# Dense stages of a four-layer graph network on one core: two operand buffers, statistics that run along, layer norms in three parts, and a Gelu on turned nodes

## The chip, the cores and the metric

The kernel runs on one core of a Trainium2 chip. Its time is the time on the device in microseconds (us), the median of several executions. The core has a matrix engine (TensorE, PE in the rows, with its weight loads as PEld), VectorE (DVE), ScalarE (ACT), GpSimd (POOL) and SyncE (SP, which here only starts transfers). Each engine works through its own queue in order and waits on counters (semaphores) of the others.

## The reference

Four graph layers follow each other on 6250 nodes of 128 numbers and 100,000 edges, each with a residual and a layer norm behind it. Cut to what matters here:

```python
x = _layernorm(x + L0(x, ...))   # edge means; three times relu(out @ W.T + b), then a batch norm over all nodes
x = _layernorm(x + L1(x, ...))   # relu((mean of neighbours + x) @ W.T + b)
x = _layernorm(x + L2(x, ...))   # messages [x[src], x[dst]] @ Wmsg[type]; mean; then the lines below
x = _layernorm(x + L3(x, ...))   # weighted sum of neighbours @ W, + b, relu, batch norm

# inside L2
h = jnp.concatenate([x, agg], axis=-1) @ Wupd + bupd
mu = jnp.mean(h, axis=-1, keepdims=True); var = jnp.var(h, axis=-1, keepdims=True)
hn = (h - mu) / jnp.sqrt(var + EPS) * gamma + beta
return x + jax.nn.gelu(hn, approximate=False)
```

A layer norm takes mean and variance over the 128 numbers of a node, a batch norm over the 6250 nodes of each column.

## The kernel before

**Data.** The nodes lie in `X` as 49 groups of 128 nodes: a node is a partition, its 128 numbers lie along it. A tile is one group, 128x128. Dense work goes in 7 steps (STEPS) of 7 tiles (STEP), 896 numbers wide. `A`, `B` and `sums` are three regions of one large buffer (`big` in the rows), `At` and `Bt` are views of the first two by group. `zr` and `zt` hold one step each; `zr2` and `zt2` are two more, inside `ring_raw`, which outside the dense stages is the ring of rows on their way from or to DRAM. PSUM (`ps`) has eight banks of 512.

**Stages.** The kernel sorts the edges into blocks of slots, then alternates: `gather` sends node rows to the blocks (PE with one-hot matrices, ACT, and POOL's scattering transfers), `reduce` sums blocks into nodes (SP's loads, DVE's one-hot matrices, PE, DVE's adds). Between a reduce and the next gather stands a dense stage. There are four:

- *First layer.* `edge_means` on DVE writes a step into `zr`. PE turns it (`turn`, seven transposes into banks 0 and 1, L1230), ACT copies the turned step to `zt` (`copy_t`, L826), PE multiplies halves of 448 columns into banks 2 and 3 (`mlp0`, L1237 and L1239), ACT applies bias and relu into `A` (`relu_cols`, L831), where nodes now lie turned, columns as partitions. `batch_norm` on DVE then takes 25 column statistics of 250 nodes (`column_stats`, L1666), joins them (L1676), ACT takes the square root (L836), four operations on one column each give scale and shift (L1680 to L1683), and one operation scales all of `A` (L1688). Two sublayers, mlp1 and mlp2 (L1253), do the same without the turning. In stage x1 ACT applies the last batch norm tile by tile into `zr` (L854), PE turns it back, DVE adds it to `X` (L1696) and takes each tile's norm statistics (L1607). `variances` (L1621 to L1627) and `scales` (L1635, L1636), with a square root on ACT between them (`ln_sqrt`, L869), give the factors, and DVE normalises 49 tiles (L1645).
- *f1 and g2.* f1 is the dense part of L1, g2 makes three messages per node for L2. f1: DVE's operands (L1726), turn, copy, product (`dense`, L1274), bias (L1733), relu and residual (L1735), statistics, and per step `variances` and `scales`. g2 follows two steps behind: ACT normalises a step into `zr2` (L900), turn, copy to `zt2` (L893), product (L1290) into banks 6 and 7 in turn, and DVE's add of the bias (L1750) into `msgs`, which SP writes to `msg_rows` step by step (L514). After the seventh of these transfers SP loads the first six lane rows into `zr` and `zt` (L522), from which DVE compares the one-hot matrices of the next gather (L1583).
- *f2 and Gelu.* f2: operands (L1791), turn, copy, product (L1274), add (L1798), statistics and per-step `variances` and `scales`; ACT normalises (L878), POOL multiplies by gamma and adds beta over 896 columns (L707, L709), ACT applies Gelu in a loop (L979), DVE adds it to the doubled node (L1821) and takes statistics.
- *f3 and x3*, the last layer: as mlp0 and x1, with the statistics already following the steps (L1848 for the operands, L1342 for the product); then the last norm, on DVE and ACT together, and the output.

The order within each engine is the order in which its part of the program is written.

## Time and profile before

| | us |
|---|---|
| median of 3 executions | 4178.9 |
| lowest and highest | 4169.08 and 4180.64 |
| the profiled execution | 4188.61 |
| its span, first to last instruction | 4186.9 |
| PE busy (matmuls) | 3063.3, 73% |
| DVE busy | 2712.8, 65% |
| POOL busy | 1880.8, 45% |
| ACT busy | 1166.1, 28% |

The busy shares are means over stages with different limits. Beside them the profile gives the busy time of each engine in a stretch of time (windows), the instructions in order of time (timeline) and groups of instructions by line. A row of the windows gives, behind the length, the busy time and the number of records of PE, PEld, DVE, ACT and POOL in this order, then the granted clock, the busy share of the DMA engines and GB/s. In a row of the timeline a time in brackets is idle time of the engine just before, with the instruction that ended it. Rows of the same line on the same engine that follow closely are merged, with their number as x7. A product in 32 bits appears as two records. The granted clock of PE is given in parts of 2.4 GHz: 1.00 is 2.4 GHz and 0.50 is 1.2 GHz.

### The profile page before, as it was taken

Reading aid. Unit: us, or ns where it says so; the run is one execution under the profiler, and the core shown is the slowest. Engines: PE = TensorE matmul, PEld = TensorE weight load, DVE = VectorE, ACT = ScalarE, POOL = GpSimd, SP = SyncE. Lnnn points to the kernel's source line nnn. Section 1 sums busy time; section 2 is a strip of 40 time slices with the busy share of each in tenths; the row PEclk is TensorE's granted clock in tenths of the full one; section 3 lists DMA queues with packets and bytes.
Section 4 is the critical chain, followed back from the end, with each engine's and each line's share of the span. In section 5 each row is a group of like instructions: output and inputs, shape, how many; then the busy total and the mean of one; then the engine's idle time right before and its main releaser. Section 6 shows DMA issues by size and latency. Waiting matters only on the chain.

```text
span 4186.9 us, 97803 instructions
## 1 busy us (share of the span) xinstructions
PE 3063.3 (73%) x24223; PEld 2679.1 (64%) x24224; DVE 2712.8 (65%) x7131; ACT 1166.1 (28%) x4154; POOL 1880.8 (45%) x1861
## 2 busy tenths in 40 slices
PE   7455444444388846998887799999989847998885
PEld 6233222222277616987877598899977837887883
DVE  6566766666577746665777644444467876666886
ACT  0111000000011125664112232222233047997004
POOL 3777777777600203775000166666633035773000
PEclk9999999999999977999999899999999978999997
DMA  6444444444477502444774354445466813445882
GB/s 192 145 140 145 147 144 142 147 146 140 126 240 243 162 0 88 174 180 154 235 226 153 129 150 145 147 148 153 119 186 203 257 32 128 173 178 178 252 253 76
DMA packets 423935, 667.68 MB, mean 159 GB/s; under 512 B 69406, under 2 KB 233641, under 8 KB 422873
## 3 DMA queue, kind: packets, MB, share of 16 engines
q1 hardware_dynamic: 330344, 431.37, 34.4%
q0 software_dynamic: 93552, 235.88, 15.7%
q8 instruction: 14, 0.23, 0.0%
q14 instruction: 25, 0.20, 0.0%
HBM read 418.34 MB, written 294.50 MB: 170 GB/s over the span
## 4 chain that ended last, share of the span: by engine, by line
PE 41%; POOL 20%; issue 14%; DVE 8%; DMA 7%; ACT 5%; DVEq 3%; SPq 2%; ACTq 1%; POOLq 0%
POOL slots L603 17%; PE ps L1147 15%; PE ps L1184 9%; PE ps L1188 9%; DVE hot_raw L1544 3%; ACT ring_raw L794 2%; DMA gbuf<-ring_raw,fetch_idx 2%; DMA ring_raw<-slots 2%; DMA ring_raw<-gbuf 2%; PE ps L1169 2%; PE ps L1030 2%; DVEq L409 1%; PE ps L1230 1%; POOL gbuf L649 1%; PE ps L1221 1%
## 5 line engine op out<-in xcount | busy, mean ns | idle before, releaser
L1147 PE MATMUL ps<-ring_raw,hot_raw 128*128 128x128 f32 (+2 forms) x8256 | 1012.6, 280 | 213.1 <-DVE hot_raw L1544 190.7
L1147 PEld LDWEIGHTS ps<-ring_raw,hot_raw 128*128 128x128 f32 x8256 | 966.2, 193 | 270.0 <-DVE hot_raw L1544 182.1
L649 POOL DMA_INDIRECT gbuf<-ring_raw,idx_blk x738 | 742.0, 1005 | 872.3 <-ACT fetch_idx L805 431.9
L603 POOL DMA_INDIRECT slots<-ring_raw,idx_edges x782 | 760.8, 973 | 240.9 <-issue 240.6
L1184 PE MATMUL ps<-big,hot_raw 128*128 x5328 | 613.9, 277 | 51.2 <-ACT ring_raw L797 28.7
L1184 PEld LDWEIGHTS ps<-big,hot_raw 128*128 128x128 f32 x5328 | 603.2, 193 | 62.4 <-issue 62.4
L1589 DVE TENSOR_SCALAR hot_raw<-ps,row_t 128x512 f32<-128x512 f32 x516 | 386.9, 750 | 262.3 <-PE ps L1169 260.8
L1555 DVE TENSOR_TENSOR big<-big,ps 128x128 f32 (+2 forms) x1032 | 292.4, 283 | 246.4 <-PE ps L1147 243.6
L1544 DVE SCALAR_TENSOR_TENSOR hot_raw<-ring_raw,back,lane_ids 128x512 f32<-128x512 f32 x516 | 386.1, 749 | 74.9 <-DMA ring_raw<-slots 40.8
L1062 PE MATMUL ps<-big 128*49 128x343 bf16 (+6 forms) x784 | 264.1, 490 | 206.3 <-DVE big L1444 205.2
L1544 DVE SCALAR_TENSOR_TENSOR hot_raw<-dst_key,back,lane_ids 128x512 f32<-128x512 f32 x516 | 388.8, 754 | 9.0 <-PE ps L1184 4.0
L1062 PEld LDWEIGHTS ps<-big 128*49 128x49 bf16 x784 | 113.9, 159 | 349.8 <-DVE big L1444 169.1
L1071 PE MATMUL ps<-big 49*128 49x98 f16 x784 | 159.7, 256 | 233.5 <-ACT big L729 233.5
L1188 PE MATMUL ps<-X,hot_raw 128*128 x2064 | 289.0, 283 | 24.7 <-DVE hot_raw L1589 16.8
L1188 PE MATMUL ps<-big,hot_raw 128*128 x2064 | 288.7, 283 | 23.7 <-ACT ring_raw L794 12.1
L794 ACT ACTIVATE ring_raw<-ps,pays_raw 128x128 f32<-128x128 f32 x1032 | 293.8, 375 | 0.0
L1583 DVE TENSOR_SCALAR hot_raw<-zr,row_t 128x512 f32<-128x512 bf16 x333 | 150.7, 507 | 214.9 <-PE ps L1184 208.3
L797 ACT COPY ring_raw<-ps 128x512 f32<-128x512 f32 x480 | 278.8, 583 | 0.0
L1188 PEld LDWEIGHTS ps<-X,hot_raw 128*128 128x128 f32 x2064 | 251.6, 192 | 31.7 <-issue 31.4
L1188 PEld LDWEIGHTS ps<-big,hot_raw 128*128 128x128 f32 x2064 | 251.3, 192 | 30.6 <-issue 30.4
L1071 PEld LDWEIGHTS ps<-big 49*128 49x128 f16 x784 | 103.4, 136 | 258.5 <-issue 258.5
L788 ACT COPY idx_blk<-to_blk 128x1 uint32 (+1 forms) x738 | 143.4, 194 | 436.6 <-PE ps L1184 266.1
(249 smaller groups left out, 3824.6 us busy)
## 6 DMA issues: line engine op xcount, KB each, us to landing
ring_raw<-gbuf SPq DMA_DIRECT2D x774, 268.0 KB, 3.3
ring_raw<-slots SPq DMA_DIRECT2D x258, 272.0 KB, 3.5
ring_raw<-in_edge_attr SPq DMA_DIRECT2D x111, 448.0 KB, 4.0
pays_raw<-key_rows SPq DMA_DIRECT2D x112, 224.0 KB
zr<-lane_rows SPq DMA_DIRECT2D x111, 128.0 KB, 3.6
zt<-lane_rows SPq DMA_DIRECT2D x111, 128.0 KB, 3.3
big<-src_rows SPq DMA_DIRECT2D x112, 112.0 KB
slots<-ring_raw,idx_edges POOLq DMA_INDIRECT x782
```

What stands on the lines that cost most here:

```text
L603: pool.indirect_dma_start(edges, bass.IndirectOffsetOnAxis(idx_edges[0:n, u, j:j + 1], 0), edge_rows[0:n, u, j, :], None).then_inc(scatter ...
L649: pool.indirect_dma_start(gbuf, bass.IndirectOffsetOnAxis(idx_blk[:, r:r + 1], 0), node_rows[:, r, :], None, bounds_check=NBLK - 1, oob_is ...
L794: ins = act.activation(rows[:, j, 0:D], parts[:, j, :], ACT.Copy, scale=pays_raw[:, bass.ds(at * (BLK * PAY) + (j * PAY + P_W), 1)])
L797: ins = act.copy(rows[:, :, 0:D], parts)
L1062: ins = pe.matmul(counts_of(s)[:, j * GROUPS:].rearrange("p (n g) -> p n g", g=GROUPS), hot2[:, s, 0, :, j], hot2[:, s, 1, :, j][:, None, ...
L1071: pe.matmul(to, hot, bases[:, s, 0, :], start=True, stop=False, skip_group_check=True)
L1147: ins = pe.matmul(bank(r % 3, width), hots[:, r, j * P:(j + 1) * P], rows[:, j, 0:width], start=j == 0, stop=j == BLK - 1)
L1184: ins = pe.matmul(to, hots3[:, r % 2, t, j * P:(j + 1) * P], msgs_flat[:, bass.ds(at[r] + t * D, D)], start=t == 0, stop=t == TYPES - 1)
L1188: ins = pe.matmul(to, hots[:, r, j * P:(j + 1) * P], nodes[:, bass.ds(at[r], D)], start=True, stop=True)
L1544: dve.scalar_tensor_tensor(out=hots[:, r, :].rearrange("p (k d) -> p k d", k=BLK), in0=key.broadcast_to([P, BLK, P]), scalar=back[:, k, ba ...
L1555: dve.tensor_tensor(to, to, bank(r % 3, width), ALU.add).then_inc(added, 1)
L1589: ins = dve.tensor_scalar(hots[:, r, :], bank(r % 3), row_t[:, 1:2], None, ALU.is_equal)
```

## The change

The gather and reduce stages stay as they are. In the dense stages:

1. mlp0 and f3 get two buffers for turned operands (`turned_to`: `zt` and `zt2`) and four product banks (2 to 5) instead of two; ACT's copy of the next step stands ahead of the relus of this one (`turned_layer`).
2. Column statistics of mlp0, mlp1 and mlp2 wait for the halves that they need (`columns_of`), and in mlp0 they stand between the operand sets (`layer_operands`), as in f3 before. The scaling of `A` is cut into 14 halves, each of which releases one product.
3. In x1 and x3 ACT applies the batch norm in one activation per step, into `zr` and `zt` in turn; PE turns into banks 0 to 1 and 2 to 3 in turn; DVE's statistics follow one step behind the adds. After x1 ACT normalises 3 of 7 tiles of each step, DVE 4.
4. The twelve turns of `lanes_t` and their copy stand between mlp1 and mlp2. POOL, not DVE, zeroes `sums` before the first graph layer.
5. The layer norms behind f1 and f2 take `variances`, square root and `scales` for steps 0 to 1, 2 to 4 and 5 to 6 (`CHUNKS`) and no longer per step. g2 follows three steps behind f1, not two.
6. SP loads the first six lane rows ahead of the last three transfers of messages.
7. POOL's multiply and add are gone. PE turns the normalised steps into PSUM (`z_turn`), ACT applies Gelu to them with gamma and beta as scale and bias columns (`cols[:, 13:15]`), PE turns them back (`g_turn`), and DVE adds them from PSUM. DVE normalises the last two steps.
8. Loops over the 7 steps are mostly written out.

Three places of the order. On DVE between the last operands of mlp0 and the statistics of mlp1, before:

```order
L1664 MEMSET big 128x6517 [waits mlp0_z]
L1666 BN_STATS bn_st<-big 128x6 [waits mlp0_r]
L1666 BN_STATS bn_st<-big 128x6 x24
L1676 BN_AGGR bn_mv<-bn_st 128x2 [waits vector_chain]
L1680 RECIPROCAL bn_c<-bn_c 128x1 [waits bnsd_in,bnsd_out]
L1681 TENSOR_TENSOR bn_c<-bn_c,cols 128x1 [waits vector_chain]
L1682 TENSOR_TENSOR bn_c<-bn_mv,bn_c 128x1 [waits vector_chain]
L1683 TENSOR_TENSOR bn_c<-cols,bn_c 128x1 [waits vector_chain]
L1688 TENSOR_SCALAR big<-big,bn_c 128x6272 [waits vector_chain]
L1666 BN_STATS bn_st<-big 128x6 [waits mlp1_r]
L1666 BN_STATS bn_st<-big 128x6 x24
```

and now:

```order
L1701 BN_STATS bn_st<-big 128x6 [waits mlp0_r] x4
L1697 TENSOR_SCALAR zr<-big,rcnt 128x128 [waits mlp0_t]
L1697 TENSOR_SCALAR zr<-big,rcnt 128x128 x6
L1701 BN_STATS bn_st<-big 128x6 [waits mlp0_r] x11
L1729 BN_AGGR bn_mv<-bn_st 128x2 [waits vector_chain]
L1733 RECIPROCAL bn_c<-bn_c 128x1 [waits bnsd_in,bnsd_out]
L1734 TENSOR_TENSOR bn_c<-bn_c,cols 128x1 [waits vector_chain]
L1735 TENSOR_TENSOR bn_c<-bn_mv,bn_c 128x1 [waits vector_chain]
L1736 TENSOR_TENSOR bn_c<-cols,bn_c 128x1 [waits vector_chain]
L1743 TENSOR_SCALAR big<-big,bn_c 128x448 [waits vector_chain]
L1743 TENSOR_SCALAR big<-big,bn_c 128x448 x13
L1701 BN_STATS bn_st<-big 128x6 [waits mlp1_r] x25
```

The memset is gone from DVE. The eleven last statistics of mlp0 wait one by one for its relus, and the 25 of mlp1 stand behind fourteen scaled pieces.

On ACT from the end of f2 (normalising `big`) through Gelu, before:

```order
L878 ACTIVATE big<-big,nmr,rstd 128x128 [waits f2_scaled]
L878 ACTIVATE big<-big,nmr,rstd 128x128 x6
L981 UNCONDITIONAL_BRANCH
L981 ISA
L979 ISA [waits norm_ready]
L979 ACT_TABLE_LOAD
L979 ACTIVATE big<-big 128x896
L981 REGISTER_ALU
L981 COMPARE_AND_BRANCH
L869 ACT_TABLE_LOAD
L869 ACTIVATE sd<-mv,eps_col 128x49 [waits mv_done]
```

and now:

```order
L882 ACTIVATE sd<-mv,eps_col 128x21 [waits mv_done]
L833 COPY zt<-ps 128x896 [waits f2_t,f2_m]
L894 ACTIVATE big<-big,nmr,rstd 128x128 [waits f2_scaled]
L894 ACTIVATE big<-big,nmr,rstd 128x128 x20
L882 ACTIVATE sd<-mv,eps_col 128x14 [waits mv_done]
L1013 ACT_TABLE_LOAD
L1013 ACTIVATE zr<-ps,cols 128x896 [waits z_turned]
L1013 ACTIVATE zt<-ps,cols 128x896 [waits z_turned]
L1013 ACTIVATE zr<-ps,cols 128x896 [waits g_turned,z_turned]
L1013 ACTIVATE zt<-ps,cols 128x896 [waits g_turned,z_turned]
```

The table load stands ahead of the first Gelu and no longer in a loop; the last square root stands behind 21 activations.

On SP, messages (`msg_rows`) and lane rows, before:

```order
L498 COMPARE_AND_BRANCH
L514 DMA msg_rows<-big 128x7x384 [waits g2_r] x7
L518 UNCONDITIONAL_BRANCH [waits f1_m,lane_rows_out]
L518 ISA
L522 ISA [waits src_hots]
L522 DMA zr<-lane_rows 128x512
L520 REGISTER_ALU
```

and now:

```order
L506 COMPARE_AND_BRANCH
L534 DMA msg_rows<-big 128x7x384 [waits g2_r] x4
L524 DMA zr<-lane_rows 128x512 [waits src_hots,lane_rows_out,f1_m]
L524 DMA zr<-lane_rows 128x512 [waits src_hots] x2
L524 DMA zt<-lane_rows 128x512 [waits src_hots] x3
L534 DMA msg_rows<-big 128x7x384 [waits g2_r] x3
L536 UNCONDITIONAL_BRANCH
```

Six lane loads now stand between the fourth and the fifth transfer of messages.

The diff, cut to its core by engine. Lines taken away are mostly left out, since the functions they were in stand above.

Constants and buffers:

```diff
+CHUNKS = ((0, 2), (2, 5), (5, 7))
+CHUNK_OF = [c for c, (a, b) in enumerate(CHUNKS) for _ in range(a, b)]
...
+        turned_to = (zt_flat, zt2_flat)
```

SP, the messages and lane rows:

```diff
+                    for i in range(STEPS):
+                        if i == STEPS - 3:
+                            sp.wait_ge(lane_rows_out, 16)
+                            sp.wait_ge(st["f1"]["m"], STEPS)
+                            load_lanes(0)
+                        sp.wait_ge(st["g2"]["r"], NEAR + (i + 1) * STEP)
+                        sp.dma_start(table[:, i * STEP:(i + 1) * STEP, :],
+                                     msgs[:, i * STEP:(i + 1) * STEP, :]).then_inc(msgs_out, 16)
+                    with sp.Fori(1, MIXR + 1) as i:
+                        load_lanes(i)
```

POOL, at the head of its blocks, and what is gone behind f2:

```diff
+            pool.wait_ge(st["mlp0"]["z"], GROUPS)
+            pool.memset(sums_flat, 0.0).then_inc(sums_zero, 1)
...
-            for i in range(STEPS):
-                t = Bt[:, i * STEP:(i + 1) * STEP, :]
-                pool.wait_ge(b_normed, (i + 1) * STEP)
-                pool.tensor_tensor(t, t, bc[:, 0:1, :].broadcast_to([P, STEP, D]), ALU.mult).then_inc(scaled_b, 1)
-                pool.wait_ge(scaled_b, i + 1)
-                pool.tensor_tensor(t, t, bc[:, 1:2, :].broadcast_to([P, STEP, D]), ALU.add).then_inc(
-                    norm_ready, 1)
```

ACT, the order of the turned layers, x1, its norm, f1 with g2, f2 with Gelu:

```diff
+            def turned_layer(stage, bias):
+                copy_t(stage, 0, turned_to[0])
+                for i in range(STEPS):
+                    if i + 1 < STEPS:
+                        copy_t(stage, i + 1, turned_to[(i + 1) % 2])
+                    relu_cols(stage, i, bias)
...
+                    act.activation((zr_flat, zt_flat)[i % 2], A[:, i * STEP * D:(i + 1) * STEP * D], ACT.Identity,
+                                   bias=bn_c[:, k, 3:4], scale=bn_c[:, k, 2:3]).then_inc(st[stage]["z"], STEP)
...
+            act.wait_ge(y_scaled, 1)
+            for i in range(STEPS):
+                normalise_step(X, i, x1_ready, Y_CUT)
...
+            next_copy("f1", 1)
+            next_copy("f1", 2)
             ln_sqrt(2, 0)
+            next_copy("f1", 3)
             g2_operands(0)
+            g2_copy(0)
+            next_copy("f1", 4)
+            g2_operands(1)
+            g2_copy(1)
+            next_copy("f1", 5)
             ln_sqrt(2, 1)
...
+            g2_operands(2)
+            g2_copy(2)
+            next_copy("f1", 6)
+            g2_operands(3)
+            g2_copy(3)
+            g2_operands(4)
+            ln_sqrt(2, 2)
+            g2_copy(4)
+            g2_operands(5)
+            g2_copy(5)
+            g2_operands(6)
+            g2_copy(6)
...
+            next_copy("f2", 3)
+            act.wait_ge(f2_scaled, 1)
+            normalise_step(Bt, 0, b_normed)
+            next_copy("f2", 4)
+            normalise_step(Bt, 1, b_normed)
+            next_copy("f2", 5)
+            ln_sqrt(3, 1)
+            next_copy("f2", 6)
+            act.wait_ge(f2_scaled, 2)
+            for i in range(*CHUNKS[1]):
+                normalise_step(Bt, i, b_normed)
+            ln_sqrt(3, 2)
+            for i in range(STEPS):
+                act.wait_ge(z_turned, i + 1)
+                if i > 1:
+                    act.wait_ge(g_turned, i - 1)
+                act.activation((zr_flat, zt_flat)[i % 2], tslots((4, 2)[i % 2]), ACT.Gelu, bias=cols[:, 14:15],
+                               scale=cols[:, 13:14]).then_inc(gelu_done, 1)
```

PE, with `turned_layer` for mlp0 and f3 and `turn_back` for x1 and x3:

```diff
+            def product_bank(stage, n):
+                if n >= 4:
+                    pe.wait_ge(st[stage]["r"], n - 3)
+                return bank(2 + n % 4, HALF)
+            def turned_layer(stage, product):
+                turn(stage, 0)
+                for i in range(STEPS):
+                    pe.wait_ge(st[stage]["c"], i + 1)
+                    if i + 1 < STEPS:
+                        turn(stage, i + 1)
+                    for h in range(2):
+                        n = 2 * i + h
+                        product(product_bank(stage, n), n, turned_to[i % 2][:, h * HALF:(h + 1) * HALF]).then_inc(
+                            st[stage]["m"], 1)
...
+                for n in range(2 * STEPS):
+                    pe.wait_ge(bn_applied, (k - 1) * 2 * STEPS + n + 1)
+                    pe.matmul(product_bank(stage, n), wT[:, 2 + k, :], A[:, n * HALF:(n + 1) * HALF],
+                              start=True, stop=True).then_inc(st[stage]["m"], 1)
+                if k == 1:
+                    pe.wait_ge(lanes_ready, 4)
+                    for q in range(LTURNS):
+                        ins = pe.transpose(lanes_turned[:, q, :], lanes_t[:, q * LCOLS:(q + 1) * LCOLS], ident_h[:, :])
+                    ins.then_inc(turned_lanes, 1)
+            def turn_back(stage):
+                for i in range(STEPS):
+                    if i > 1:
+                        pe.wait_ge(st[stage]["r"], i - 1)
+                    turn(stage, i, (zr, zt)[i % 2], (0, 2)[i % 2])
...
+                if i > 2:
+                    g2_turn(i - 3)
                 pe.wait_ge(st["f1"]["r"], i)
                 dense("f1", wT[:, 5, :], i)
+                if i > 2:
+                    g2_wide(i - 3)
...
+            g2_wide(STEPS - 4)
+            for i in range(STEPS - 3, STEPS):
+                g2_turn(i)
+                g2_wide(i)
...
+            def z_turn(i):
+                if i < CHUNKS[2][0]:
+                    pe.wait_ge(b_normed, (i + 1) * STEP)
+                else:
+                    pe.wait_ge(norm_ready, (i + 1 - CHUNKS[2][0]) * STEP)
+                if i == 1:
+                    pe.wait_ge(st["f2"]["r"], STEPS)
+                if i > 1:
+                    pe.wait_ge(gelu_done, i - 1)
+                for j in range(STEP):
+                    ins = pe.transpose(tslot(j, (4, 2)[i % 2]), Bt[:, i * STEP + j, :], ident[:, :])
+                ins.then_inc(z_turned, 1)
+            def g_turn(i):
+                pe.wait_ge(gelu_done, i + 1)
+                if i > 1:
+                    pe.wait_ge(gelu_added, i - 1)
+                for j in range(STEP):
+                    ins = pe.transpose(tslot(j, (6, 0)[i % 2]), (zr, zt)[i % 2][:, j, :], ident[:, :])
+                ins.then_inc(g_turned, 1)
+            z_turn(0)
+            for i in range(STEPS):
+                if i + 1 < STEPS:
+                    z_turn(i + 1)
+                g_turn(i)
```

DVE:

```diff
+            def columns_of(stage, first, end):
+                for n in range(first, end):
+                    dve.wait_ge(st[stage]["r"], -(-(n + 1) * BN_COLS // HALF))
+                    ins = column_stats(n)
+                return ins
+            def layer_operands(stage, operands):
+                done = 0
+                for i in range(STEPS):
+                    if i:
+                        dve.wait_ge(st[stage]["t"], i)
+                    operands(i)
+                    if i > 1:
+                        end = (i - 1) * STEP * P // BN_COLS
+                        columns_of(stage, done, end)
+                        done = end
+                return done
+            means_done = layer_operands("mlp0", edge_means)
...
+                for n in range(2 * STEPS):
+                    t = A[:, n * HALF:(n + 1) * HALF]
+                    dve.tensor_scalar(t, t, c[:, 2:3], c[:, 3:4], ALU.mult, ALU.add).then_inc(bn_applied, 1)
...
+                for i in range(STEPS):
                     dve.wait_ge(st[stage]["t"], i + 1)
+                    dve.tensor_tensor(step_of(X, i), step_of(X, i), grouped(tslots((0, 2)[i % 2])), ALU.add).then_inc(
                         st[stage]["r"], 1)
+                    if i:
+                        dve.wait_ge(st[stage]["r"], i)
+                        group_stats(X, i - 1)
+                dve.wait_ge(st[stage]["r"], STEPS)
+                group_stats(X, STEPS - 1)
...
+            for i in range(STEPS):
+                for j in range(Y_CUT):
...
+            for i in range(STEPS):
+                f1_results(i)
+                if i == CHUNKS[0][1]:
+                    f1_scales(0)
+                if i + 2 < STEPS:
+                    f1_operands(i + 2)
+                f1_stats(i, i - 3 if i > 2 else None)
+                if i + 1 == CHUNKS[CHUNK_OF[i]][1]:
+                    variances(CHUNK_OF[i])
+                    if CHUNK_OF[i] == 1:
+                        f1_scales(1)
+            g2_results(STEPS - 3)
+            f1_scales(2)
...
+            for i in range(STEPS):
+                f2_results(i)
+                if i in (CHUNKS[0][1], CHUNKS[1][1]):
+                    f2_scales(CHUNK_OF[i] - 1)
+                if i + 2 < STEPS:
+                    f2_operands(i + 2)
                 dve.wait_ge(st["f2"]["r"], i + 1)
                 group_stats(Bt, i)
+                if i + 1 == CHUNKS[CHUNK_OF[i]][1]:
+                    variances(CHUNK_OF[i])
+            scales(2)
+            wait(chain.last())
...
+            for i in range(STEPS):
+                dve.wait_ge(g_turned, i + 1)
+                dve.scalar_tensor_tensor(out=step_of(X, i), in0=step_of(X, i), scalar=2.0,
+                                         in1=grouped(tslots((6, 0)[i % 2])), op0=ALU.mult, op1=ALU.add).then_inc(
+                    gelu_added, 1)
+                if i:
+                    dve.wait_ge(gelu_added, i)
+                    group_stats(X, i - 1)
+            dve.wait_ge(gelu_added, STEPS)
+            group_stats(X, STEPS - 1)
```

## Rows read from the trace of the kernel before

**Rows 1.** Windows by stage: length, busy us per engine, granted clock, DMA.
```profile
1434.00:1614.00 180.00, 85.18 (x220) 39.99 (x219) 99.31 (x260) 54.45 (x103) 23.51 (x19) 0.68 0.00 0
...
1614.00:2273.00 659.00, 574.86 (x5167) 552.48 (x5165) 440.38 (x857) 255.61 (x1033) 251.21 (x258) 0.98 0.58 192
...
2273.00:2382.00 109.00, 72.84 (x294) 45.89 (x294) 75.38 (x230) 33.23 (x71) 0.00 (x0) 0.85 0.27 95
...
3366.00:3475.00 109.00, 33.38 (x147) 27.76 (x147) 85.05 (x256) 53.07 (x100) 35.24 (x15) 0.63 0.00 0
...
4103.00:4187.00 84.00, 35.84 (x128) 19.99 (x126) 52.73 (x172) 42.99 (x93) 0.00 (x0) 0.69 0.14 38
```

**Rows 2.** Timeline, mlp0: start us, us, engine, line, operation, idle before, releaser.
```profile
1467.13 0.90 ACT L826 COPY zt<-ps 128x896 f32<-128x896 f32 x1
...
1472.91 0.90 ACT L826 COPY zt<-ps 128x896 f32<-128x896 f32 x1
...
1483.63 8.10 DVE L1666 BATCH_NORM_STATS2 bn_st<-big 128x6 f32<-128x250 f32 x25 [5.45 <-ACT big L831]
...
1493.73 3.55 DVE L1688 TENSOR_SCALAR big<-big,bn_c 128x6272 f32<-128x6272 f32 x1
...
1497.34 3.35 PE L1253 MATMUL ps<-big,wT 128*128 128x448 f32 x4 [14.41 <-DVE big L1688]
```

**Rows 3.** Timeline of stage 1: early operands, second scaling, x1, norm.
```profile
1444.01 6.03 DVE L1656 TENSOR_SCALAR zr<-big,rcnt 128x128 f32 x7 [0.79 <-PE ps L1230]
...
1530.77 3.54 DVE L1688 TENSOR_SCALAR big<-big,bn_c 128x6272 f32<-128x6272 f32 x1
...
1569.38 2.81 ACT L854 ACTIVATE zr<-big,bn_c 128x128 f32<-128x128 f32 x7 [0.81 <-DVE bn_c L1683]
...
1577.77 1.80 DVE L1607 BATCH_NORM_STATS2 stats<-X  x7
...
1599.38 13.73 DVE L1645 TENSOR_SCALAR X<-X,rstd,nmr  x49 [0.37 <-DVE nmr L1636]
```

**Rows 4.** Windows of 5 us in stage 1: mlp0, mlp1, x1.
```profile
1465.00:1470.00 5.00, 3.31 (x14) 1.85 (x13) 1.04 (x6) 2.06 (x3) 0.00 (x0) 1.00 0.00 0
...
1510.00:1515.00 5.00, 3.53 (x8) 1.35 (x8) 0.00 (x0) 2.25 (x4) 0.00 (x0) 1.00 0.00 0
...
1585.00:1590.00 5.00, 3.62 (x13) 2.02 (x12) 4.09 (x14) 3.87 (x10) 0.00 (x0) 0.50 0.00 0
```

**Rows 5.** Timeline of f1/g2 and the start of the second gather.
```profile
2293.00 1.75 PE L1230 MATMUL ps<-ident,zr 128*128 128x128 f32 x7 [4.06 <-ACT zt L826]
...
2331.29 5.24 PE L1290 MATMUL ps<-wcat,ring_raw 128*128 128x384 f32 x10 [3.21 <-DVE big L1750]
...
2373.88 0.56 DVE L1750 TENSOR_TENSOR big<-ps,bc 128x384 f32<-128x384 f32 x1 [0.36 <-PE ps L1290]
...
2382.43 18.48 PE L1184 MATMUL ps<-big,hot_raw 128*128 x144 [8.59 <-DVE hot_raw L1583]
```

**Rows 6.** Timeline of f2 and of the last statistics behind Gelu.
```profile
3382.07 1.92 DVE L1791 SCALAR_TENSOR_TENSOR zr<-big,rcnt 128x128 f32 x7
...
3391.39 1.92 DVE L1791 SCALAR_TENSOR_TENSOR zr<-big,rcnt 128x128 f32 x7
...
3422.28 2.03 DVE L1627 SCALAR_TENSOR_TENSOR mv<-mv,sd 128x7 f32<-128x7 f32 x1
...
3460.78 1.68 DVE L1607 BATCH_NORM_STATS2 stats<-X  x7
```

**Rows 7.** Groups of the third dense stage: busy us, mean ns | idle before.
```profile
L979 ACT ACT_TABLE_LOAD x7 | 9.0, 1283 | 0.1
```

**Rows 8.** Timeline of f3: two copies and the last statistics.
```profile
4116.10 0.90 ACT L826 COPY zt<-ps 128x896 f32<-128x896 f32 x1
...
4120.30 0.90 ACT L826 COPY zt<-ps 128x896 f32<-128x896 f32 x1
...
4136.32 2.66 DVE L1666 BATCH_NORM_STATS2 bn_st<-big 128x6 f32<-128x250 f32 x8 [6.43 <-ACT big L831]
```

289 lines of the change are left out of this document (73 added, 216 removed).

## The prediction

> **What bounds the kernel now.** I read the windows by stage first [rows 1]. Four dense stages (the first layer's network, f1/g2, f2 with Gelu, f3 with the last norm) take 180, 109, 109 and 84 us, 482 of a span of 4187. There no engine is full: in the first PE is busy 85 of 180 us, DVE 99, ACT 54; in the third PE has 33 of 109. The rest is mostly gather and reduce, where PE is busy 575 of 659 us, and which the diff leaves alone. So the dense stages are chains of waits, and what they gain goes straight to the end. Then the timeline. In mlp0 one step of seven node groups recurs every 5.78 us (copies at 1467.13 and 1472.91) [rows 2], while PE is busy 3.31 of 5 us, so 3.8 per step [rows 4]: the single operand buffer makes PE and ACT take turns. Behind the last relu DVE does all 25 column statistics in 8.10 us, then one 3.55 us scaling of all nodes, and only then does PE start again [rows 2].
>
> **Stage 1, first layer.** *mlp0.* With two buffers and four product banks a step costs PE's 3.8 us plus a handshake, 3.9. The first operand sets stay slow beside POOL's list work (6.03 us, where 1.92 is undisturbed) [rows 3, 6]; after those, five steps at 3.9 instead of 5.8 save 9.5. Statistics run behind the relus: about 2 of 25 (0.65 us) are left after the last one, instead of 8.10. Going through the queues in order, the scaling that now starts at 1493.73 [rows 2] starts at about 1476: **18 us**.
> *mlp1, mlp2.* From one scaling to the next is 37.0 us, and from there to x1's first activation 38.6 (1493.73, 1530.77, 1569.38) [rows 2, 3]. New: DVE scales 14 pieces. With a fixed cost near 0.3 (13.73 us for 49 small ones is 0.28 each [rows 3]) and the slope 3.55/6272 a piece of 448 is 0.47, so 6.6 us; then 25 statistics, 8.1; 14.7 in one queue. PE needs 14 products of 448 columns. Four records took 3.35 us at 1.2 GHz [rows 2], two make a product, so 1.5 us with what lies between them, and 0.75 at 2.4 GHz. PE idled 14.41 us before them; now about 4. It may still start at the lower level, but is then fed without holes. I take 5 us at 1.2 GHz: 13 us in all, under DVE's 14.7. With 2.0 us of aggregate and column arithmetic (from 1491.73, the end of the statistics, to 1493.73) that is 16.7 per layer against 37.0 and 38.6: **42 us**.
> *x1, norm.* From the first activation to the normalising is 30.0 us [rows 3]; ACT's seven small activations are 2.81 us a step and PE's turns and DVE's add follow them. One wide activation costs about a wide copy, 0.90 [rows 2]. DVE's add (1.1, as for f1's results) and statistics (1.80) then bound the step: 3 + 7 x 2.97 = 23.8, plus some 2.6 of norm arithmetic, 26.4: **3.6**. Normalising moves from DVE alone, 13.73 us, to 28 tiles on DVE (7.8) beside 21 on ACT (21 x 2.81/7 = 8.4): **5.3**. The 12 turns of lane rows move into a PE wait between mlp1 and mlp2: **1** (seven turns take 1.75 at this level [rows 5]; twelve narrow ones lie between 0 and 3). Priced at nothing: zeroing the sums goes from DVE to POOL, and both wait there; the lane rows leave 80 us earlier than ACT's new wait for them; loops written out, of which no row shows a cost; two more column loads at the start, under the edge lists. Sum **70**.
>
> **Stage 2, f1/g2.** The per-step variances and their sqrt round trips go, but the three parts add waits. g2's operands for steps 2 to 4 all wait for part 1, which is ready only after step 4's statistics; then ACT needs 2.8 us, PE a turn (1.75 for seven [rows 5], or half of it), and f1's product for step 5 stands behind that turn in PE's queue with DVE waiting for it: about 5 us idle, once. Steps 5 and 6 wait for part 2, whose scale now stands in DVE's queue behind seven g2 results. Two whole g2 steps of 8 to 9 us then follow each other with nothing beside them. Now PE waits 3.21 us in a middle step until DVE gets to its g2 results, and its next ten records spread over 5.24 us [rows 5]. Going through DVE, PE and ACT in order I reach the last g2 result at 2379 where it was 2373.88: a loss of 5.5. Against this the first lane rows are loaded three message transfers earlier: PE started 8.0 us after that last result (8.59 us idle) [rows 5] and would need only three compares, 1.5: 6.5 back. **Net 1 gained.** Bounds: 6 lost (PE at 1.2 GHz in the middle steps), 6 gained (the 5 us are filled).
>
> **Stage 3, f2 and Gelu.** POOL's multiply and add go. Beside them a tiny DVE operation takes 2.03 us, and steps lie 9.3 us apart (operands at 3382.07 and 3391.39) [rows 6]. New steps are a product (3.0), an add (1.1) and the operands with the turn behind them (2.3): 6.5. So f2's last product ends near 3411, and ACT, which first normalises steps 2 to 4 (8.4 us), reaches its last sqrt at 3417; DVE does the last 14 tiles till 3422. Gelu then reads turned nodes from PSUM, with one table load instead of seven of 1.28 us [rows 7]: ACT about 1 us a step, PE two turns, DVE 1.1 + 1.7. PE's turns decide: in x1 the granted clock stayed at 0.50, the 1.2 GHz level, through a stretch of nothing but turns [rows 4], where seven take 1.75 [rows 5]. From 3422 the last eleven, 1.85 each with the handshake, end at 3442, and add and statistics at 3445, where they ended at 3462.5 [rows 6]: **17**.
> The Trainium skill (TensorE: Matmul & The Clock Gate, Part 4: PE-mode transpose) says that turns in transpose mode don't count as activity for the clock. By that rule this term is 17; if they counted, the eleven turns would take 11 us, DVE at 2.8 us a step would bound it, and the term would be 18. The row of x1 agrees with the rule, though PE had holes there.
>
> **Stage 4, f3, x3.** f3's steps are 4.2 us (4116.10, 4120.30) [rows 8]. With two buffers DVE's queue binds: operands 1.93 and three or four statistics 1.2, so 3.3. Some seven steps' worth gives 6.3 at the last relu, and 2 of statistics behind it instead of eight in 2.66 us [rows 8]: 8.3. x3 as x1, 4.2 with its somewhat shorter statistics. Sum **12.5**. The last normalising and the output stay.
>
> **Sum.** 70 + 1 + 17 + 12.5 = 100.5 us. The profiled execution took 4188.6 (span 4186.9), so 4088, a ratio of 0.976; on the median 4178.9 that is **4078**.
>
> **Rivals.** (a) *The clock stays low in mlp1 and mlp2.* For: PE started at 1497.34 and the granted clock is 1.00 only in the window from 1510 [rows 2, 4]. Against: it had a hole in each step, which goes. Price: 14 x 1.5 + 0.5 + 3.5 = 25 per layer instead of 16.7, 16.5 in all: 4095.
> (b) *f1/g2 eats more.* Part 1 comes late, the two bare g2 steps run at 1.28 instead of 0.78 a tile (7 us), and the lane rows save less, because the last message transfer, on which POOL waits, leaves no earlier (6): +1 becomes -12, 4091.
> (c) *The change does little of what it says.* zr remains a single operand buffer between DVE and PE, so mlp0, f2 and f3 keep their cadence. Then statistics (24), pieces and clock (20), norm and lanes (6), x1 and x3 (5) and Gelu (8) remain: 63, 4116. Against: 1.92 us of operands fit under PE's products.
> (d) *Slower than before.* PE has fewer rests; if the clock fell in gather and reduce, 10 us at 1.2 GHz would cost 5 where PE is full. From 200 us of new low clock on there is nothing left of the gain; 240 us would give 4198. Against: the stretch shows 0.98 [rows 1] at 87% busy, and its work doesn't change.
>
> **How the numbers follow.** Forecast 0.6, (a) 0.17, (b) 0.13, (c) 0.06, (d) 0.01, a better end than the bounds below 0.03. The likeliest gives 4078. Down, f1/g2 with its 5 us filled, Gelu at the higher level (1), f2's steps shorter by 1 us each (6) and scaled pieces at 0.3 instead of 0.47 us (2 x 2.4) give 17: 4061. Up, (a) and (b) are each inside 4095, and both together give 4107: range 4060 to 4108, with (c) and (d) outside. A measurement of this kernel tells about 0.3%, 12.5 us, from no change: faster 0.97, same 0.02, slower 0.01.
>
> **What would show it.** In the new profile: mlp0's copies 3.9 us apart; from mlp1's first scaled piece to mlp2's 16.7 us with DVE never idle (25 and a clock of 0.50 would be rival a); 0.65 us of statistics after each last relu; x1's steps 3 us; one DVE wait of about 5 us for f1's product of step 5, the last g2 result 106 us after the stage's start and PE 1.5 us behind it; one Gelu table load, PE full beside Gelu at 0.50; f3's steps 3.3. I am wrong if a dense stage keeps its length, or if gather and reduce change by more than 5 us each.

## The result, and the profile after

The changed kernel takes 4067.6 us (median of 4 executions, 4058.54 to 4073.64) where the kernel before takes 4178.3: a ratio of 0.974 with a 95% interval of 0.9719 to 0.9762, 110.8 us less. Forecast were 4078 and a range of 4060 to 4108. The profiled execution took 4058.54 us (span 4056.7), the shortest of the four, and that of before (4188.61) lies above all four of its kernel; so 19 us of the 130 between the two traces are not the change's, and lengths are compared stage by stage.

The windows of the changed kernel answer to [rows 1]: four lines are the dense stages, and the third is the longest gather with the reduce behind it.

```profile
1438.00:1538.00 100.00, 65.93 (x222) 37.48 (x222) 84.22 (x259) 52.70 (x83) 27.19 (x19) 0.81 0.01 3
...
2188.00:2299.00 111.00, 80.05 (x294) 50.16 (x294) 70.02 (x192) 32.68 (x66) 0.00 (x0) 0.83 0.24 85
2299.00:3280.00 981.00, 904.42 (x7539) 861.93 (x7539) 540.81 (x1177) 236.38 (x775) 495.16 (x478) 0.99 0.55 169
3280.00:3368.00 88.00, 48.53 (x256) 41.28 (x257) 68.86 (x241) 39.39 (x76) 5.53 (x1) 0.72 0.00 0
...
3992.00:4057.00 65.00, 31.00 (x126) 19.71 (x126) 49.42 (x172) 31.38 (x51) 0.00 (x0) 0.73 0.18 50
```

The first stage is 100 us and no longer 180, the third 88 and no longer 109; the second is 2 us longer than it was. To compare kernels, I take each stage from its first operands on DVE to the first product of the gather behind it, each gather from its first to its last product, each reduce from there to the next operands (the last stage to the start of the last normalising operation on DVE):

| us | before | after | change | forecast |
|---|---|---|---|---|
| stage 1: to the first scaling | 57.8 | 37.1 | -20.7 | -18 |
| mlp1 and mlp2 | 75.7 | 32.9 | -42.8 | -42 |
| x1 to the normalising | 30.0 | 22.2 | -7.8 | -3.6 |
| norm and lane turns | 16.6 | 10.1 | -6.5 | -6.3 |
| stage 2, f1/g2 | 107.5 | 111.2 | +3.7 | -1 |
| stage 3, f2 and Gelu | 110.9 | 88.1 | -22.8 | -17 |
| stage 4, f3 and x3 | 75.6 | 56.4 | -19.2 | -12.5 |
| the four stages | | | -116.0 | -100.5 |
| second reduce (behind f1/g2) | 327.4 | 336.9 | +9.5 | 0 |
| third reduce | 292.9 | 288.2 | -4.7 | 0 |

The four stages are summed before rounding. -116.0 + 9.5 - 4.7 is -111.2, against 110.8 of the medians. What else differs between the two traces is the first reduce (8.9 us shorter) and the second gather (11.8 us shorter). On the same chip the kernels of e2, e4, e10 and e11, which don't touch these two, differ from the changed kernel by up to 8.6 and 9.6 us there, so most of it is spread.

The timeline of mlp0 to x1, as [rows 2, 3] (start, length, engine, line, operation, idle before; DVEq and PEq are the sequencers of these engines):

```profile
1461.61 0.91 ACT L833 COPY ring_raw<-ps 128x896 f32<-128x896 f32 x1
...
1465.39 0.91 ACT L833 COPY zt<-ps 128x896 f32<-128x896 f32 x1
...
1474.82 6.01 DVE L1743 TENSOR_SCALAR big<-big,bn_c 128x448 f32<-128x448 f32 x14
1475.39 12.29 PE L1278 MATMUL ps<-big,wT 128*128 128x448 f32 x28 [4.02 <-DVE big L1743]
...
1480.74 8.38 DVE L1701 BATCH_NORM_STATS2 bn_st<-big 128x6 f32<-128x250 f32 x25
...
1491.13 6.01 DVE L1743 TENSOR_SCALAR big<-big,bn_c 128x448 f32<-128x448 f32 x14
...
1507.70 1.13 ACT L867 ACTIVATE zr<-big,bn_c 128x896 f32<-128x896 f32 x1 [0.87 <-DVE bn_c L1736]
```

Copies are 3.78 us apart (forecast 3.9, before 5.78). DVE goes from 14 scaled pieces to 25 statistics without a hole, 16.3 and 16.6 us per layer (forecast 16.7). PE does all 14 products in 12.29 us, hidden under DVE. In x1 a step is now 2.35 us:

```profile
1514.32 1.07 DVE L1750 TENSOR_TENSOR X<-X,ps 128x896 f32<-128x896 f32 x1
1514.35 1.13 ACT L867 ACTIVATE zt<-big,bn_c 128x896 f32<-128x896 f32 x1
1515.31 1.44 DVE L1649 BATCH_NORM_STATS2 stats<-X 128x6 f32<-128x128 f32 x7
...
1516.67 1.07 DVE L1750 TENSOR_TENSOR X<-X,ps 128x896 f32<-128x896 f32 x1
```

f1/g2 and the start of the second gather, as [rows 5]:

```profile
2250.08 1.10 DVE L1791 TENSOR_TENSOR ps<-ps,bc 128x896 f32<-128x896 f32 x1 [6.39 <-PE ps L1302]
...
2277.01 2.80 ACT L919 ACTIVATE ring_raw<-X,nmr,rstd 128x128 f32<-128x128 f32 x7 [7.92 <-DVEq L1813]
...
2296.71 0.56 DVE L1807 TENSOR_TENSOR big<-ps,bc 128x384 f32<-128x384 f32 x1 [0.36 <-PE ps L1318]
...
2299.01 16.34 PE L1208 MATMUL ps<-big,hot_raw 128*128 x144 [2.34 <-DVE hot_raw L1625]
```

Both new waits of the forecast are there: DVE stands 6.39 us for f1's product of step 5 (5 forecast), and ACT 7.92 us for the last scale, which DVE has queued behind seven g2 results. The last g2 result comes 108.9 us behind the stage's first operands, where it was 99.0. PE follows 2.3 us later instead of 8.5.

f2 and Gelu, as [rows 6]:

```profile
3315.51 5.53 POOL L720 MEMSET big<- 128x6517 f32 x1 [155.74 <-DVE zr L1849]
...
3317.39 3.68 DVE L1667 TENSOR_SCALAR mv<-mv 128x21 f32<-128x21 f32 x1
...
3330.89 0.29 ACT L882 ACTIVATE sd<-mv,eps_col 128x14 f32<-128x14 f32 x1
...
3336.68 1.70 PE L1382 MATMUL ps<-ident,zt 128*128 128x128 f32 x7
...
3341.50 0.93 PE L1374 MATMUL ps<-ident,big 128*128 128x128 f32 x7
...
3351.16 2.80 DVE L1649 BATCH_NORM_STATS2 stats<-X 128x6 f32<-128x128 f32 x14
```

The last square root starts 50.5 us behind the stage's first operands (51 forecast). Seven turns take 1.70 us at first and 0.93 later: the clock rises while PE does nothing but turns, which the forecast had not expected.

The length of this stage isn't fixed by the program. In e3 and e6, which change nothing in it, it takes 85.0 us and not 88.1. There the clock is at its upper level in the first 16 us of f2, and a step's product takes 1.73 us where it takes 2.9 to 3.2 in the changed kernel. The windows of the changed kernel and of e3 (behind the busy times of the five engines stands the granted clock):

```profile
3280.00:3296.00 16.00, 11.29 (x50) 8.89 (x50) 9.97 (x34) 2.71 (x3) 0.00 (x0) 0.79 0.00 0
```

```profile
3299.00:3315.00 16.00, 11.78 (x70) 8.44 (x70) 12.89 (x49) 2.72 (x3) 0.00 (x0) 1.00 0.00 0
```

In the changed kernel, e3, e5, e6, e8 and e10, which all have the same stage, it takes 85.0 to 89.0 us, so a difference of less than 4 us in its length tells nothing by itself.

### The profile page after: what moved, and what is told of

Same layout as the page of the kernel before. It is cut to its first block, busy times and chain, and to the rows that moved or that the text cites. A ratio compares the mean times of both kernels' runs of the same rounds, so it can differ in the third digit from the quotient of the medians.

```text
span 4056.7 us, 96019 instructions
## 1 busy us (share of the span) xinstructions
PE 3057.3 (75%) x24321; PEld 2686.8 (66%) x24322; DVE 2674.3 (66%) x7085; ACT 1137.4 (28%) x4063; POOL 1851.6 (46%) x1848
## 3 DMA queue, kind: packets, MB, share of 16 engines
q0 software_dynamic: 93552, 235.88, 16.1%
## 4 chain that ended last, share of the span: by engine, by line
PE 41%; POOL 21%; issue 13%; DVE 8%; DMA 7%; ACT 4%; DVEq 3%; SPq 2%; ACTq 1%; POOLq 0%
POOL slots L616 18%; PE ps L1171 15%; PE ps L1212 9%; PE ps L1208 8%; DVE hot_raw L1586 3%; DMA gbuf<-ring_raw,fetch_idx 2%; ACT ring_raw L802 2%; PE ps L1193 2%; DMA ring_raw<-slots 2%; DMA ring_raw<-gbuf 2%; PE ps L1054 2%; DVEq L417 1%; POOL gbuf L662 1%; PE ps L1249 1%; SPq L417 1%
## 5 line engine op out<-in xcount | busy, mean ns | idle before, releaser
L1212 PE MATMUL ps<-big,hot_raw 128*128 x2064 | 289.6, 284 | 24.3 <-DVE hot_raw L1631 15.9
L802 ACT ACTIVATE ring_raw<-ps,pays_raw 128x128 f32<-128x128 f32 x1032 | 292.2, 379 | 0.4 <-issue 0.2
L1212 PEld LDWEIGHTS ps<-X,hot_raw 128*128 128x128 f32 x2064 | 251.8, 193 | 29.4 <-issue 29.3
```

Source lines behind the costliest of these rows:

```text
L802: ins = act.activation(rows[:, j, 0:D], parts[:, j, :], ACT.Copy, scale=pays_raw[:, bass.ds(at * (BLK * PAY) + (j * PAY + P_W), 1)])
L1212: ins = pe.matmul(to, hots[:, r, j * P:(j + 1) * P], nodes[:, bass.ds(at[r], D)], start=True, stop=True)
```

## The experiments

All lengths are read as in the table above. e1 to e4 and e9 to e11 ran on one chip, on which the kernel before took 4182.1 and 4182.7 us. e5 to e8 ran on a second (before: 4816.6) and e12 on a third (4906.8), where the gathers are longer; the dense stages are not (last section), so lengths of dense stages are compared across chips and times only with the kernel before on the same one.

**e1: early lane rows and a written-out loop, on the kernel before.**

```diff
+                        if i == STEPS - 3:
+                            load_lanes(0)
...
-                with dve.Fori(0, STEPS) as i:
+                for i in range(STEPS):
                     dve.wait_ge(st[stage]["t"], i + 1)
```

> The kernel before with two parts of the change alone. (1) SP loads the first six lane rows ahead of the last three message transfers. Theory: PE starts the second gather 2.3 us behind the last g2 result, as in the changed kernel, not 8.5: 6.2 us gained. Rival: the messages' last transfer lands no earlier, so the same time comes back inside the gather and reduce that follow (984 us from PE's start to f2's first operands would become 990). (2) the loop of x1 and x3 (DVE's add and statistics) is written out, nothing else in it. Theory: the registers of the loop cost, seven statistics fall from 1.69 to 1.44 us and the hole before them closes, so a step of 3.47 us becomes about 3.1 and both stages lose 2.5 us. Rival: the step is PE's turn and ACT's copy, and stays at 3.47. In all 4178 - 11 = 4167 by the theories, 4178 by the rivals.

Measured: 4181.2 us, ratio 0.9997 (0.9986 to 1.0009). PE starts 2.3 us behind the last g2 result and the stage has 100.4 us instead of 107.5; the time does not show it. The loop is worth next to nothing (29.4 us from the first activation to the normalising, not 30.0, where 2.5 were expected). Seven statistics take 1.45 us, not 1.80, the step is 3.47 us as it was, and DVE waits the longer for PE:

```profile
1581.58 1.09 DVE L1701 TENSOR_TENSOR X<-X,ps 128x896 f32<-128x896 f32 x1 [0.91 <-PE ps L1235]
1582.70 1.45 DVE L1612 BATCH_NORM_STATS2 stats<-X 128x6 f32<-128x128 f32 x7
...
1585.06 1.09 DVE L1701 TENSOR_TENSOR X<-X,ps 128x896 f32<-128x896 f32 x1 [0.90 <-PE ps L1235]
```

What bound a step is in the rows of ACT and PE. The kernel before, and then e1:

```profile
1583.27 2.80 ACT L854 ACTIVATE zr<-big,bn_c 128x128 f32 x7 [0.66 <-PE ps L1230]
1584.51 2.08 PE L1230 MATMUL ps<-ident,zr 128*128 128x128 f32 x7 [1.39 <-DVE X L1696]
```

```profile
1581.68 2.81 ACT L859 ACTIVATE zr<-big,bn_c 128x128 f32 x7 [0.67 <-PE ps L1235]
1582.81 2.21 PE L1235 MATMUL ps<-ident,zr 128*128 128x128 f32 x7 [1.26 <-DVE X L1701]
```

ACT needs 2.80 us for its seven activations into the one buffer `zr`, PE's last turn ends 0.5 us behind the last of them, and only then may ACT begin again: 2.80 and 0.67 are the 3.47. In e1 PE is idle 0.13 us less before its turn and takes 0.13 us longer over it, and it ends at the same distance behind ACT. So the banks that PE and DVE share did not bind in the kernel before; ACT on one buffer did.

The missing 7 us stand in the reduce behind, which takes 336.7 us, not 327.4; the third reduce gives back 4.3 of them (288.6 us, not 292.9). Groups of PE in the second reduce, the kernel before and then e1:

```profile
L1147 PE MATMUL ps<-ring_raw,hot_raw 128*128 128x128 f32 x2064 | 252.3, 279 | 32.9 <-DVE hot_raw L1544 27.0 <-DMA ring_raw<-gbuf 5.9
```

```profile
L1152 PE MATMUL ps<-ring_raw,hot_raw 128*128 128x128 f32 x2064 | 251.3, 278 | 43.0 <-DVE hot_raw L1549 37.2 <-DMA ring_raw<-gbuf 5.8
```

The work is the same and PE waits 10 us more for DVE. e9 and e10 go after that.

**e2: f1/g2 back to one norm per step and a lag of two; POOL's memset in pieces.**

```diff
-MV_COUNT = (1, len(CHUNKS), len(CHUNKS), 1, 1)
+PARTS = {2: [(i, i + 1) for i in range(STEPS)], 3: CHUNKS}
+MV_COUNT = (1, STEPS, len(CHUNKS), 1, 1)
...
+                f1_stats(i, i - 2 if i > 1 else None)
+                variances(i)
+                f1_scales(i)
...
+            for i in range(STEPS):
+                pool.wait_ge(st["f2"]["z"], (i + 1) * STEP)
+                ins = pool.memset(sums[:, i * STEP:(i + 1) * STEP, :], 0.0)
```

> The changed kernel with f1/g2 back at one variance, square root and scale per step and g2 two steps behind (written out, early lane rows kept), and POOL's memset of the sums in f2 cut into seven pieces, each behind the operands of its step. Theory: the hole in f1/g2 comes from the three parts; the last g2 result falls from 108.9 to 99 us behind the stage's first operands. Rival: it is the lower clock or the two last bare steps, and stays above 105. Memset: DVE's small multiply of 3.68 us beside it falls back to 0.2, and the last product of f2 comes 3.5 us earlier; rival: PE and ACT are late anyway and less than 1 us is seen. In all 4067 - 13 = 4054; by the rivals 4066.

Measured: 4054.6 us, 0.9695 (0.9679 to 0.9712). The last g2 result comes 95.8 us behind the first operands (99 expected): the three parts, with the lag of three steps that goes with them, cost 13.1 us there. f2 and Gelu take 85.4. The second reduce is 327.0 us long in this kernel, the third 292.2.

**e3: one part undone per stage.**

```diff
+                    dve.tensor_scalar(A[:, :], A[:, :], c[:, 2:3], c[:, 3:4], ALU.mult, ALU.add).then_inc(
+                        bn_applied, 2 * STEPS)
...
+                if k == 2:
+                    dve.wait_ge(st[stage]["r"], 2 * STEPS)
...
+                        if stage == "f3":
+                            act.wait_ge(st[stage]["m"], 2 * (i + 1))
...
+            f1_scales(2)
             g2_results(STEPS - 3)
-            f1_scales(2)
```

> The changed kernel with one part undone in each stage. mlp1: A is scaled in one operation (3.55 us) instead of 14: from its start to the next scaling 16.3 becomes 19.9 if the pieces are worth the time until PE starts, 16.3 if DVE's queue alone decides. mlp2: all column statistics behind the last relu: 16.6 becomes 24.4. x1: each step's statistics behind its own add: a step of 2.35 becomes 2.65, not 3.47, if most of the old step was the loop and the single bank. f1: the last scale ahead of g2's results of step 4: ACT starts on step 5 some 8 us earlier, and the last result comes 2.5 us earlier (106.4 behind the stage's start), since PE's queue holds the turn back until the products of step 4. f3: one buffer for turned operands: steps of 2.95 become 4.2, 7.5 us more until the last relu; rival: DVE's queue binds and the second buffer is worth under 2 us. In all 4067 + 18 = 4085.

Measured: 4082.5 us, 0.9767 (0.9751 to 0.9783).

```profile
1476.61 3.54 DVE L1746 TENSOR_SCALAR big<-big,bn_c 128x6272 f32<-128x6272 f32 x1
...
1496.47 6.01 DVE L1751 TENSOR_SCALAR big<-big,bn_c 128x448 f32<-128x448 f32 x14
1510.23 8.10 DVE L1703 BATCH_NORM_STATS2 bn_st<-big 128x6 f32<-128x250 f32 x25 [7.75 <-ACT big L838]
```

mlp1 with one scaling: 19.9 us, as expected, 3.6 more than with pieces. mlp2 with its statistics behind: 23.9 until x1 (24.4 expected), 7.4 more. So of some 21 us per layer the statistics that run along carry 7.4, the pieces 3.6, and the other ten come from PE, which needed 23 us for its 14 products before. Two of its seven pairs there:

```profile
1505.84 3.35 PE L1253 MATMUL ps<-big,wT 128*128 x4 [0.90 <-ACT big L831]
1510.10 1.76 PE L1253 MATMUL ps<-big,wT 128*128 x4 [0.90 <-ACT big L831]
```

PE stood 0.90 us behind each pair until ACT had emptied both banks, and three pairs (four in mlp2) took 3.35 us at 1.2 GHz where the others took 1.76. No run undoes these two by themselves. x1 with each step's own statistics is 0.6 us longer (2 expected). The scale ahead of g2's results gives 5.5 us (2.5 expected): I had not seen that DVE's own results of step 4 are not delayed by it while ACT gains all eight. f3 with one buffer takes 29.9 us until x3, not 25.4, in steps of 3.48 (4.2 and 7.5 us more were expected): the buffer is worth 4.5 us of the 12.0 that this part gained (37.3 before). The rest is left for the copy that stands ahead of the relus and for four banks; which of them, no run shows.

**e4: what raises the clock.**

```diff
+            pe.wait_ge(st["x1"]["r"], STEPS)
+            for j in range(72):
+                pe.transpose(ps[:, 4, 0:P], ident[:, :], ident[:, :])
...
+            for j in range(36):
+                pe.matmul(ps[:, 4, 0:P], ident[:, :], ident[:, :], start=True, stop=True)
```

> The changed kernel with 72 turns (transposes of 128x128) on PE and nothing else behind x1's last add, and 36 products of 128 columns (72 records) behind Gelu's last add, both into an unused bank while DVE and ACT normalise. Theory from the trace of the changed kernel, where the granted clock rose to 1.00 inside x1 and Gelu with turns alone on PE: the 72 turns bring the clock up as the products do, and take some 12 us. Rival (the Trainium skill, TensorE: Matmul & The Clock Gate, Part 4: PE-mode transpose, by which turns don't count as activity): the clock stays at 0.50 through all turns, which take 18 us, and rises only beside the products. The gathers that follow start a few us later.

Measured: 4092.0 us in one execution. Timeline row and windows of 2 us of the 72 turns:

```profile
1530.56 10.63 PE L1295 MATMUL ps<-ident 128*128 128x128 f32 x72 [2.94 <-DVE X L1757]
...
1532.00:1534.00 2.00, 2.00 (x11) 2.00 (x10) 1.93 (x12) 0.00 (x0) 0.00 (x0) 0.50 0.00 0
1534.00:1536.00 2.00, 2.00 (x12) 2.00 (x11) 1.37 (x7) 0.74 (x2) 0.00 (x0) 0.54 0.00 0
1536.00:1538.00 2.00, 2.00 (x21) 2.00 (x20) 2.00 (x10) 2.00 (x7) 0.00 (x0) 1.00 0.00 0
```

They take 10.6 us and the clock goes from 0.50 to 1.00 (1.2 to 2.4 GHz) while nothing but turns runs. The 72 records of products take 9.93 us, with the same rise. The Trainium skill says that turns in transpose mode don't bring TensorE up to its full clock (TensorE: Matmul & The Clock Gate, Part 4: PE-mode transpose). Page and measurement differ here, and the measurement decides.

**e5: four more parts undone, read from the lengths.**

```diff
-                if n >= 4:
-                    pe.wait_ge(st[stage]["r"], n - 3)
-                return bank(2 + n % 4, HALF)
+                banks = 2 if stage == "mlp1" else 4
+                if n >= banks:
+                    pe.wait_ge(st[stage]["r"], n - banks + 1)
+                return bank(2 + n % banks, HALF)
```

> The changed kernel with one more part undone in each stage, read from the stage lengths. mlp0: one buffer for turned operands, the copy still ahead of the relus: PE does products (3.0), waits for the copy (0.9 and 0.3), turns (0.9): steps of 5.1 instead of 3.78, 5 to 6 us more until the first scaling (37.1 becomes 43). mlp1: two product banks instead of four: each product waits for the relu two before it, 0.93 a product instead of 0.75, but DVE's queue of 14.4 us still decides: 16.3 becomes 17 at most; if banks were what made 23 us of PE's 14 products in the kernel before, it becomes 20 or more. x1: one set of banks for turned nodes: the step is DVE's add and PE's turn in turn, 3.4 instead of 2.35, so 22.2 becomes 28 to 29, which would be all of the gain there. x3: seven small activations a step instead of one: ACT's 2.81 replaces DVE's 2.35: 20.05 becomes 23.5 to 24.

Measured: 4733.4 us in one execution. mlp0 with one buffer: 42.3 us instead of 37.2, as expected. mlp1 with two banks: 19.0 instead of 16.5, more than expected (17 at most) and less than the 20 that would have put PE's old 23 us down to the banks; PE's products take 14.97 us instead of 12.48 and DVE's last statistics wait for them. x1 with one set of banks: 26.8 instead of 22.5, less than expected (28 to 29). Its steps are 2.93 us, DVE's add and PE's turn one after the other, with the clock at 0.50:

```profile
1855.52 1.75 PE L1257 MATMUL ps<-ident,zr 128*128 128x128 f32 x7 [1.18 <-DVE X L1759]
```

So of the 7.8 us in x1 ACT's wide activation and second buffer carry 3.5 (steps of 3.47 become 2.93), and the second set of banks the other 4.3, since the one set would bind next. x3 with seven small activations: 3.4 us more (3.5 to 4 expected).

**e6 and e8: early lane rows undone, and the changed kernel again.**

```diff
-                        if i == STEPS - 3:
-                            load_lanes(0)
...
+                    with sp.Fori(0, MIXR + 1) as i:
```

> The changed kernel with the first lane rows loaded behind the last message transfer again. Theory: PE and POOL both start the second gather 6.2 to 6.8 us later, and nothing catches up: 4067 becomes 4073.5, ratio to the changed kernel 1.0016. Rival, from the kernel before with this part alone, which was 7 us shorter in its stage and no faster in all: the reduce behind that gather is 327 or 337 us long, by how its loops fall into step, and the 6 us are given back there: 4067, ratio 1.000.

> The changed kernel once more, unchanged. Beside e6_lanes_late it gives the worth of the early lane rows on one chip. Its trace shows whether the lengths of the reduce stages (314.8, 336.9 and 288.2 us in the first trace of it, 323.6, 327.4 and 292.9 in that of the kernel before) belong to the kernel or to the execution: if to the kernel, they come back within 2 us; if to the execution, the second is between 327 and 337.

Measured: e6 4726.2 us, 0.9796 (0.9768 to 0.9824); e8 4708.5, 0.9777 (0.9754 to 0.9800). The intervals overlap, so the time does not decide; in the traces the stage has 117.5 us with late rows and 110.0 with early ones, and the reduce behind it 338.0 and 337.9. So an early gather does not make its reduce wait. And the lengths belong to the kernel: the second and third reduce of the changed kernel are 336.9 and 288.2 us on one chip, 337.9 and 286.4 on another.

**e7: POOL's memset in pieces alone.** The edit is the last of e2's.

> The changed kernel with POOL's memset of the sums in f2 cut into seven pieces. DVE's small multiply, 3.68 us beside the whole memset, is 0.2 again, and from f2's first operands to the last square root on ACT 50.5 becomes 47 us; the stage 88.1 becomes 84.6 to 85.4. If the memset is not what blocked DVE, 50.5 stays.

Measured: 4718.7 us in one execution. DVE's small multiply is 0.17 us again, the last square root starts 48.1 us behind the first operands, not 50.5, and the stage takes 85.7 instead of 88.1. The lengths alone prove little, since e3 and e6 reach 85.0 with the whole memset. But from f2's fifth add, ahead of the memset's effect, to the last square root it is 18.4 us in all seven traces of kernels with three parts and a whole memset (3312.53 to 3330.89 in the changed one), and 16.1, 15.9 and 15.5 in the three with pieces (e7, e2, e11). The memset did block DVE, and 2.2 to 2.8 of its 3.5 us were on the path.

**e9: the early lane rows alone, on the kernel before.** The first part of e1's edit.

> The kernel before with the early lane rows alone (x1 and x3 keep their loop, so DVE's program is word for word that of before). Theory (place): the reduce behind the second gather is 327 or 337 us long by where its loops stand in DVE's program, and e1_before_two moved them by 29 instructions when it wrote out x1's loop; here they stand where they stood, the reduce stays at 327 us and the last one at 293, and the 7 us of the stage are seen in the time: ratio 0.9983. Rival (giving back): the earlier gather itself makes the reduce wait, 337 us again, ratio 1.000.

Measured: 4171.8 us, 0.9980 (0.9968 to 0.9992). The second reduce is 327.2 us, the third 293.0. The gain of the early rows is real (the stage is 5.3 us shorter here, 7.1 in e1, 7.5 from e6 to e8), and it was the written-out loop of x1 that took it back in e1, by moving the loops behind it.

**e10: the changed kernel with 32 instructions that do nothing.**

```diff
+            for _ in range(32):
+                dve.sem_inc(issued, 1)
             dve.wait_ge(deg_sd, 1)
```

> The changed kernel with 32 instructions on DVE that only count up an unused semaphore, put where DVE waits for g2's products. They move the loops of the second reduce from instruction 1131 to 1163 and of the third from 1479 to 1511. By place (so far short when the loops begin at 0 to 16 or at 60 and above, counted modulo 64, long at 29 to 44), the second becomes short, 327 instead of 337 us, and the third long, 292 instead of 288: 6 us less in all, ratio 0.9725 where the changed kernel has 0.974. If place has nothing to do with it, 337 and 288 stay.

Measured: 4069.2 us, 0.9734 (0.9713 to 0.9755), not to be told from the changed kernel's 0.974 (6 us were expected, and its interval is 8 wide on each side). The trace tells it: the second reduce fell from 336.9 to 326.9, the third rose from 288.2 to 292.4, as expected of both.

**e11: the best of them.** e2 with 28 such instructions behind f2's second operands.

> The kernel of e2_steps_pieces with 28 such instructions on DVE behind f2's second operands, where it waits for PE. The second reduce stays at 327 us; the third, now from instruction 1544, becomes 288 instead of 292. Stages otherwise as in e2: 103, 98, 85 and 57 us. In all 4054 - 4 = 4050, ratio 0.9685; without an effect of place 0.9695.

Measured: 4052.0 us, 0.9692 (0.9671 to 0.9712): 15 us under the changed kernel, and not to be told from e2. The stages are 102.3, 97.6, 86.8 and 56.4 us, the second and third reduce 326.7 and 289.5.

**e12: the kernel before without POOL's multiply and add.**

```diff
-                pool.tensor_tensor(t, t, bc[:, 0:1, :].broadcast_to([P, STEP, D]), ALU.mult).then_inc(scaled_b, 1)
...
-                act.wait_ge(norm_ready, i + 1)
+                act.wait_ge(b_normed, i * STEP + STEP)
```

> The kernel before without POOL's multiply by gamma and add of beta behind f2 (these two are left out of the computation), Gelu waiting for ACT's normalising instead, all else as before: a variance and a square root per step, Gelu with its table load in the loop. It divides the 22.8 us that the third dense stage lost between POOL's part and the rest. Theory: beside POOL's two operations one small DVE operation of each of f2's steps took 1.93 us, two in the last two steps; they fall to 0.17, 9 operations by 1.8 are 16 us, less some 3 where POOL's memset of the sums now falls on DVE's work: the stage goes from 110.9 to about 97 us, and the remaining 9 us of the change are the three parts, the single table load and Gelu on turned nodes. Rival: the steps are bound by the round trip to ACT for the square root, and the stage stays over 106 us. In time 4182 - 14 = 4168, ratio 0.9967.

Measured: 4889.2 us, 0.9975 (0.9949 to 1.0000). The stage takes 97.6 us where it took 110.9 (97 expected; 110.4 and 110.8 in e1 and e9): 13.3 of the change's 22.8 us come from taking these two operations away. f2's steps are 7.3 us and no longer 9.05:

```profile
3945.19 1.09 DVE L1791 TENSOR_TENSOR big<-ps,big 128x896 f32 x1 [0.63 <-DVE nmr L1629]
...
3952.48 1.09 DVE L1791 TENSOR_TENSOR big<-ps,big 128x896 f32 x1 [0.64 <-DVE nmr L1629]
```

## Why the prediction was right, and where it was off

The range held the time and the forecast was 10.5 us too high. It had 100.5 us of gain in four dense stages; they gave 116.0, and 4.8 went elsewhere. That it came so close is in part luck. It had 7.2 us too little gain in x1 and x3, 5.8 in f2 and Gelu, 3.7 in f3 and 2.7 in mlp0; against these stand 4.7 us too much in f1/g2 and the 4.8 of the reduces, which it put at nothing.

*Steps that held.* mlp0's cadence (3.9 forecast, 3.78 measured), the statistics behind the relus, 16.7 us per layer in mlp1 and mlp2 (16.3 and 16.6), the norm on two engines and the lane turns, f2 as far as the last square root. The bound in mlp1 and mlp2 was DVE's queue, as put; e3 shows that it needs both halves of the edit. Rival (a) did not come, and its clock did only for a moment: PE's products begin at the lower level in both layers and leave it after 3 to 4 us, where the forecast had allowed for 5. In mlp2:

```profile
1492.00:1494.00 2.00, 2.00 (x4) 0.93 (x3) 2.00 (x6) 0.63 (x1) 0.00 (x0) 0.52 0.12 26
...
1496.00:1498.00 2.00, 2.00 (x6) 0.95 (x5) 2.00 (x6) 1.76 (x3) 0.00 (x0) 1.00 0.16 36
```

Nor did (c): mlp0 does 3.78 us. Nor (d): the third window above has 0.99.

*x1 and x3, 7.8 forecast, 15.0 measured.* The term was mis-sized in the price of statistics. I took 1.80 us for seven from a row of the kernel before [rows 3], where DVE was waiting for PE anyway; written out they are 1.44. "Loops written out, of which no row shows a cost" is true where DVE waits, as e1 shows, and false once DVE is the bound. The step that I put at 2.97 is 2.35, and seven of them are 4.3 us in each stage. What bound the old step the prediction has: ACT's seven activations of 2.81 us, with PE's turns behind them. That the one set of banks would bind next, at 2.93 us, is in no sentence of it; e5 shows it.

*f1/g2, 5.5 us of loss forecast, 9.9 measured.* The hole at part 1 was right (6.39 for 5). The mis-sized term is the end: two bare g2 steps of "8 to 9 us", which took 20.2 us together (2276.5 to 2296.7), the first because ACT starts only after its 7.92 us. e3 gives 5.5 of it back by one line moved, and e2 all and 3.2 more. The lane rows gave 6.2 where 6.5 were forecast. This is half of rival (b): the stage costs 3.7 us instead of gaining 1, but the rows save what they should.

*Gelu, 17 forecast, 22.8 measured.* From the last tiles of DVE to the last statistics I had 23 us by eleven turns of 1.85 at 1.2 GHz; it took 18.5 (3335.45 to 3353.96). The step that failed is that PE's turns decide at 1.2 GHz. In x1 of the kernel before and of e5 PE had a hole of 1.2 to 1.6 us in each step and the clock was at 0.50; e4 shows turns without holes raising it. In x1 of the changed kernel it rose over the first turns, which stand close, to 1.00 at 1514, and was at 0.50 again from 1520, behind steps with holes of 1.4 us. By the prediction's own working the clock is worth only 1 of these 4.5 us; the rest is DVE's step, which binds then, at 2.35 us instead of the 2.8 of the prediction, by the same statistics as in x1. The prediction gave POOL's part no price of its own; by e12 it is 13.3 us of the stage. Against this stands POOL's memset, 2.2 to 2.8 us on the path (e7), which it had not priced. The stage's own spread of 4 us lies over all of this.

*f3, 8.3 forecast, 12.0 measured.* Steps of 2.95 us instead of 3.3, and a start-up that the old order paid as well: the second copy comes 2.35 us behind the first, where it came 5.9. The buffer alone is 4.5 (e3).

*Gather and reduce, 0 forecast, +4.8 measured.* "Its work doesn't change" is right and was not enough. The second reduce is 9.5 us longer and the third 4.7 shorter than before, in the changed kernel on two chips, and e10 changes both by adding instructions that do nothing. By its own words the prediction is wrong "if gather and reduce change by more than 5 us each": for the second reduce that sign came, and the mechanism behind it was in none of the rivals.

## What to carry to other kernels

Where a stage is a chain of turns between engines, first give the shared buffer or bank a second copy, then put each engine's next hand-over ahead of its own bulk work; the parts of this kind that e3 and e5 undid are worth 0.6 to 7.4 us each. Look for the loop that binds next, too: in x1 the wide activation and the second buffer gave 3.5 of 7.8 us, and the second set of banks the rest. Grouping small operations (here the norms in three parts) pays only where nothing waits for the group's last member: in f1 it cost 13 us, and in f2 no run tests it alone. And a price that was read in a loop while the engine had time to spare is an upper bound, not a price.

## What the runs showed of the hardware

**Place of a loop.** The loops of the second and third reduce are the same instructions in every kernel here. Counting DVE's instructions from the program's start, taken modulo 64 where the loops begin:

| begins at (mod 64) | second reduce, us |
|---|---|
| 0 (before, e9) | 327.4, 327.2 |
| 11 (e10), 16 (e2, e11) | 326.9, 327.0, 326.7 |
| 29 (e1), 32 (e3) | 336.7, 338.1 |
| 43 (after, e8) | 336.9, 337.9 |

| begins at (mod 64) | third reduce, us |
|---|---|
| 60 (e3), 3 (e1), 7 (after), 8 (e11) | 289.7, 288.6, 288.2, 289.5 |
| 38 (before), 39 (e10), 44 (e2) | 292.9, 292.4, 292.2 |

The runs left out fit: e4 to e7 begin where the changed kernel does and have 336.4 to 338.0 and 285.1 to 288.4 us, e12 begins where the kernel before does and has 326.8 and 291.8. Three of the runs (e9, e10 and e11) were foretold by this count. That place decides is shown; by what mechanism is open, as is whether 64 is the right number: counted modulo 128 the long ones begin at 93 to 108 and the short ones at 0 to 71, which fits as well.

**POOL beside DVE.** Row of POOL, and of DVE in the same stretch, in e12:

```profile
3962.75 5.53 POOL L705 MEMSET big<- 128x6517 f32 x1 [158.52 <-DVE zr L1784]
```

```profile
3964.31 0.17 DVE L1614 TENSOR_TENSOR mv<-stats  x1 [0.26 <-DVE stats L1600]
...
3964.89 0.17 DVE L1617 SCALAR_TENSOR_TENSOR sd<-sd  x1
3964.97 3.33 DVE L1619 TENSOR_SCALAR mv<-mv  x1
```

A memset on POOL lets DVE's operations with two inputs pass at 0.17 us and holds a one-input TENSOR_SCALAR until it ends. POOL's multiply and add of two tensors held DVE's operations with two inputs in the kernel before (SCALAR_TENSOR_TENSOR 2.03 us [rows 6]); each TENSOR_SCALAR of DVE came only at their end there, so nothing shows what they do to one. The Trainium skill (SBUF — State Buffer, SBUF: two separate sides) says that the port pair shared by the two is locked for a whole instruction, against DVE's two-port modes by any GpSimd operation, and against DVE operations with two SBUF inputs only by one that reads SBUF. These rows agree, if TENSOR_SCALAR runs in such a mode, which no row shows.

**Chips.** On the second chip the page of the changed kernel shows a mean of 142 GB/s where the first shows 165, and the first gather takes 448.7 us instead of 332.9; its dense stages are 102.8, 110.0, 88.1 and 56.5 us, as on the first (102.3, 111.2, 88.1, 56.4). The change gave 108 us there and 111 here, so its ratio is 0.9777 on the one and 0.974 on the other.
